# Masked cross-attention layer: two pairs of PSUM banks for scores instead of three, four ring banks instead of two, and scores later in TensorE's queue

## The chip, the cores and the metric

The kernel runs on one core of a Trainium2 chip as one program. The metric is the device time of one execution in microseconds (us); lower is better.

## What is computed

Four layers run one after the other over x of shape (4, 1024, 256), with a context of 77 keys. Layer 0 is causal attention and an MLP, layer 1 linear attention with a window, layer 2 the masked cross-attention, layer 3 a cross-attention with 16 heads of 64. The change touches layer 2 only:

```python
q = (queries @ Wq.T + bq).reshape(B, Nq, h, d).transpose(0, 2, 1, 3)      # h = 16, d = 16
k = (keys @ Wk.T + bk).reshape(B, -1, h, d).transpose(0, 2, 1, 3)         # 77 keys
v = (values @ Wv.T + bv).reshape(B, -1, h, d).transpose(0, 2, 1, 3)
scores = jnp.einsum('bhqd,bhkd->bhqk', q, k) / jnp.sqrt(jnp.float32(d))
scores = scores * attention_weights
scores = jnp.where(attention_mask, -jnp.inf, scores)
p_attn = jax.nn.softmax(scores, axis=-1)
out = jnp.einsum('bhqk,bhkd->bhqd', p_attn, v)
out = out.transpose(0, 2, 1, 3).reshape(B, Nq, D)
out = out @ Wo.T + bo
x = queries + out                                                         # then a layer norm
```

## The kernel before

`masked_context` (from line 1651) computes layer 2. Its unit is a tile of 128 tokens; there are 8 in each of 4 batches. For a tile, all 16 heads times 77 keys lie side by side in one row of 1232 scores, worked in two halves m of 616. A half is a unit (b, i, m), numbered 0 to 63. The steps of a tile, each a token in the queue of its engine:

- `scores` (TensorE, line 1805): q times the block-diagonal keys `kbd`, into a pair of PSUM banks of 308 columns each. `scores_of` gives the pair, number modulo 3: banks 0 to 5.
- `take` (VectorE, line 1959): multiplies the half in place by the weights `fs`, loaded by DMA.
- `low` (TensorE, line 1816): adds the mask, made to bf16 by `lower` on ScalarE (line 1906), onto the same banks.
- `shift` (VectorE, lines 1968 and 1972): maximum of each head, then scores less maximum into `pr` in SBUF. After it the pair of banks is free.
- `exp` (ScalarE, line 1913).
- `turned`, three groups of transposes of `pr` (TensorE, line 1867; evacuated to `pT` by ScalarE, line 1939).
- `att` (TensorE, line 1877: 20 small matmuls of `pT` with the values `V`; VectorE, lines 2005 and 2008: reciprocal of the sums and product).
- `flat` (TensorE, line 1883; ScalarE, line 1945), `out` (TensorE, line 1889; VectorE adds it to x, line 2014), `stats` (VectorE, line 1978).

Once a batch come `V` (TensorE, line 1849), and for the batch after it the transposes of x, `turn` (line 1855), the projections `q` (line 1861), on GpSimd the bias and the block-diagonal `kbd` and `vbd` (lines 1786 and 1777), and for the batch before it the layer norm (lines 1558 to 1592, with its root on GpSimd). During the last batch 16 projections `next` (line 1837) for the following layer run as well.

The order of each engine's queue is fixed ahead of time: `masked_schedule` gives each token a time in units of half a tile, and each engine's list is sorted by it. A token waits only by semaphores, and every engine works its list strictly in order.

PSUM has eight banks. Six hold scores. All other TensorE results (`k`, `v`, `V`, `turn`, `q`, `turned`, `att`, `flat`, `out`, `next`) go in turn through the ring of banks 6 and 7; class `Banks` makes a token wait until the one that used its bank before, two tokens earlier, is emptied by VectorE or ScalarE. `scores` waits for the `shift` of the unit three back.

Of the kernel before, what the change touches and what calls it, by code (L numbers as in the profile page):

```python
# [278 lines left out]
def build(nc, a, out):  # L279
    with ExitStack() as whole:  # L280
# [25 lines left out]
        front_layers(nc, a, sem, start, x, ident, identb, (below, near), ctxT, banks, masked)  # L306
        clear(nc, list(sems.values())[before:])
        masked_context(nc, a, sem, masked, folded, x, ident, identb, ctxT, banks)
        folded_context(nc, a, sem, folded, masked, x, ident, ctxT, banks, out)
        clear(nc, early)  # L310
# [1181 lines left out]
def masked_schedule():  # L1492

    pe, dve, act, pool, sp = [], [], [], [], []

    def fill(time, token, engine, after=0.3):

        pe.append((time, token))
        {"v": dve, "s": act}[engine].append((time + after, token))

    for m in range(ND):
        fill(-9 + m / 10, ("k", m), "v")
        fill(-8.5 + m / 10, ("v", m), "v")
    for b in range(B):
        t0 = UNITS * b
        for m in range(ND):
            pool.append((t0 - 6.5 + m / 10 if b else -7 + m / 10, ("keys", b, m)))
            pool.append((t0 - 6 + m / 10 if b else -6 + m / 10, ("vals", b, m)))
        fill(t0 + 1.2, ("V", b), "v")
        early = t0 - 9 if b else -5  # L1510
        for half in range(2):
            for k in range(ND):
                fill(early + 2 * half + k / 2, ("turn", b, half, k), "vs"[k])
            for m in range(ND):
                fill(early + 2 * half + 1.3 + m / 2, ("q", b, half, m), "s")
            pool.append((early + 2 * half + 1.5, ("bias", b, half)))
        for i in range(NT):
            for m in range(2):
                n = t0 + 2 * i + m
                u = (b, i, m)  # L1520
                pe += [(n - 1.4, ("scores", *u)), (n + 0.3, ("low", *u))]
                dve += [(n, ("take", *u)), (n + 1.1, ("shift", *u))]
                act.append((n + 1.6, ("exp", *u)))
            at = t0 + 2 * i
            sp.append((at - 6, ("side", b, i)))
            act.append((at - 1.6, ("lower", b, i)))
            for j in range(3):
                fill(at + 3.3 + j / 5, ("turned", b, i, j), "s")
            fill(at + 4.55, ("att", b, i), "v", 0.5)
            fill(at + 5.6, ("flat", b, i), "s")  # L1530
            fill(at + 6.4, ("out", b, i), "v", 0.5)
            dve.append((at + 7.2, ("stats", b, i)))
        end = t0 + UNITS + 5.7
        if b + 1 < B:
            norm_tokens(b, end, 0.5, dve, act, pool)

    for n in range(2 * NPAIR):
        fill(57 + 0.8 * n, ("next", n), "s")
    return [[token for _, token in sorted(steps, key=lambda step: step[0])] for steps in (pe, dve, act, pool, sp)]


def norm_tokens(b, at, pace, dve, act, pool):

    dve.append((at, ("spread", b)))
    pool.append((at + 0.05, ("root", b)))
    for i in range(NT):
        dve += [(at + 1 + pace * i, ("norm", b, i)), (at + 1.6 + pace * i, ("close", b, i))]
        act.append((at + 2.2 + pace * i, ("square", b, i)))
    dve.append((at + 3 + pace * NT, ("mean", b)))
    pool.append((at + 3.05 + pace * NT, ("mean_root", b)))  # L1550
# [100 lines left out]
def masked_context(nc, a, sem, t, folded, x, ident, identb, ctxT, banks):  # L1651

    nbuf = NBUF
    RING = (6, 7)
    wq, wk, wv, wo, bq, bk_, bv, bo, gamma, beta = (t[n] for n in ("wq", "wk", "wv", "wo", "bq", "bk", "bv", "bo",
                                                                   "gamma", "beta"))
    xT, qT, kv, kbd, vbd, heads, pick, ones, V = (t[n] for n in ("xT", "qT", "kv", "kbd", "vbd", "heads", "pick", "ones",
# [1 line left out]
    fs, mk, low, pr, pT, att, attT, top, inv = (t[n] for n in ("fs", "mk", "low", "pr", "pT", "att", "attT", "top",  # L1659
                                                               "inv"))  # L1660
# [5 lines left out]
             "mean", "mean_root", "newton", "chain")  # L1666
    side = [sem(f"side{n}") for n in range(nbuf)]
    pe_order, dve_order, act_order, pool_order, sp_order = masked_schedule()
    in_ring = lambda t: t[0] in ("k", "v", "V", "turn", "q", "turned", "att", "flat", "out", "next")
    of = lambda order, *kinds: [t for t in order if t[0] in kinds]  # L1670
    ring = Banks(banks, RING, [t for t in pe_order if in_ring(t)], sem("ring_ready"),
                 (Tally(sem("emptied_v"), [t for t in dve_order if in_ring(t)]),
                  Tally(sem("emptied_s"), [t for t in act_order if in_ring(t)])))
    scored, lowed = Tally(sem("scored"), of(pe_order, "scores")), Tally(sem("lowed"), of(pe_order, "low"))
    taken, shifted = Tally(sem("taken"), of(dve_order, "take")), Tally(sem("shifted"), of(dve_order, "shift"))
# [3 lines left out]
    number = {u: n for n, u in enumerate((b, i, m) for b in range(B) for i in range(NT) for m in range(2))}  # L1679
    unit = list(number)  # L1680
# [2 lines left out]

    def scores_of(u):

        r = 2 * (number[u] % 3)
        return banks[:, r:r + 2, 0:UW // 2]

    def by_head(ap):
# [5 lines left out]
    with nc.Block() as block:  # L1695
        @block.sync
        def _(sp):
            for _, b, i in sp_order:
                n = tile_of(b, i)
                if n < nbuf:  # L1700
                    continue
                if n == NT:
                    folded_loads(sp, a, sem, folded)
                sp.wait_ge(*taken.after(("take", *tiles[n - nbuf], 1)))
                sp.wait_ge(*lowered.after(("lower", *tiles[n - nbuf])))
                side_inputs(sp, a, sem, t, b, i)
            sp.wait_ge(loaded, 16 * nload)
            for done in side:
                sp.wait_ge(done, 32 * B * NT // nbuf)
# [80 lines left out]
        def _(pe):  # L1790
            for token in pe_order:
                what, *args = token
                if what == "scores":
                    b, i, m = args
                    n = number[b, i, m]
                    if n >= 3:
                        pe.wait_ge(*shifted.after(("shift", *unit[n - 3])))
                    if i % 4 == 0:
                        pe.wait_ge(*ring.emptied(("q", b, i // 4, m)))
                    if i == 0:  # L1800
                        pe.wait_ge(*keys_ready.after(("keys", b, m)))
                    for j in range(2):

                        rows = slice(P // 2 * j, P // 2 * (j + 1))
                        ins = pe.matmul(scores_of((b, i, m))[:, j], qT[rows, b % 2, m, i * P:(i + 1) * P],
                                        kbd[rows, b % 2, m, j * UW // 2:(j + 1) * UW // 2], start=True, stop=True,
                                        skip_group_check=True)
                    ins.then_inc(sem("scored"), 1)
                    continue
                if what == "low":  # L1810
                    b, i, m = args
                    pe.wait_ge(*taken.after(("take", b, i, m)))
                    pe.wait_ge(*lowered.after(("lower", b, i)))
                    for j in range(2):
                        c0 = m * UW + j * UW // 2
                        ins = pe.matmul(scores_of((b, i, m))[:, j], identb[:],
                                        low[:, tile_of(b, i) % 3, c0:c0 + UW // 2], start=False, stop=True,
                                        skip_group_check=True)
                    ins.then_inc(sem("lowed"), 1)
                    continue  # L1820
# [10 lines left out]
                elif what == "next":  # L1831
                    n, = args
# [116 lines left out]
        def _(dve):  # L1949
            chain = Chain(dve, sem("chain"))  # L1950
            for token in dve_order:
                what, b, *args = token
                if what == "take":
                    i, m = args
                    n = tile_of(b, i)
                    dve.wait_ge(*scored.after(("scores", b, i, m)))
                    dve.wait_ge(side[n % nbuf], 32 * (n // nbuf + 1))
                    two = scores_of((b, i, m))
                    dve.tensor_tensor(two, two, half_of(fs[:, n % nbuf, :], m).rearrange("p (a c) -> p a c", a=2),
                                      ALU.mult).then_inc(sem("taken"), 1)  # L1960
                    continue
# [450 lines left out]
```

## Time and profile before

| | |
|---|---|
| median of 3 runs | 2225.31 us (2221.91 to 2230.49) |
| profiled execution, its own time | 2232.05 us |
| its span, first to last instruction | 2230.3 us |
| mean granted TensorE clock | 0.971 |
| busy share of TensorE, VectorE, ScalarE, GpSimd | 90%, 62%, 51%, 34% |
| masked layer within the span | about 1557 to 1877 us |

Times in the rows are us from the start of the span. PE is TensorE's matmuls, PEld its weight loads, DVE is VectorE, ACT ScalarE, POOL GpSimd. PEclk is the granted clock as a share of 2.4 GHz. A row with xN stands for N instructions in a run; its second number is the time from the start of the first to the end of the last.

### The profile page before, as it was taken

How to read it: one execution, taken by the hardware profiler on the slowest of the kernel's cores; microseconds unless marked ns; L12 is line 12 of the kernel's file. 1: busy time of each engine (PE TensorE's matmuls, PEld its weight loads, DVE VectorE, ACT ScalarE, POOL GpSimd, SP SyncE). 2: the span in 40 equal slices, each digit the busy share in tenths (PEclk: the TensorE clock that was granted, in tenths of full speed). 3: DMA queues.
4: the chain of work that ended last, by engine and by line, in shares of the span. 5: the costliest groups of instructions: out<-in, count | busy, mean ns of one | idle time of the engine just before them, and what ended most of it. 6: DMA issues, size and time to landing. Idle time of an engine off the chain costs nothing. (4 is left out here: it accounts for less than half of the span.)

```text
span 2230.3 us, 38605 instructions
## 1 busy us (share of the span) xinstructions
PE 2013.3 (90%) x14610; PEld 1309.0 (59%) x14610; DVE 1386.9 (62%) x3054; ACT 1137.6 (51%) x1750; POOL 769.4 (34%) x1012
## 2 busy tenths in 40 slices
PE   4999999999998879998999899998989998999989
PEld 2333433343342258876566575765666667888989
DVE  4876776685767655645545554451677884866655
ACT  2265565555545666651645545363445553555444
POOL 3023124113212353311624526253111201756656
PEclk8799999999998999998999999999999999999999
DMA  6705403510730000018460716320422210000000
GB/s 146 140 7 113 60 1 68 89 23 36 113 76 1 1 15 1 1 55 122 92 108 21 143 17 131 66 66 1 162 86 86 85 58 1 11 10 13 16 13 20
DMA packets 77774, 126.68 MB, mean 57 GB/s; under 512 B 16650, under 2 KB 34826, under 8 KB 77582
## 3 DMA queue, kind: packets, MB, share of 16 engines
q1 hardware_dynamic: 74966, 122.63, 26.0%
q8 instruction: 118, 1.93, 0.4%
q10 hardware_dynamic: 2624, 1.58, 0.2%
q14 instruction: 66, 0.54, 0.1%
HBM read 93.59 MB, written 30.32 MB: 56 GB/s over the span
## 5 line engine op out<-in xcount | busy, mean ns | idle before, releaser
L1099 DVE TENSOR_REDUCE nmx_causal<-banks 128x1 f32<-128x333 f32 (+4 forms) x896 | 435.6, 538 | 174.1 <-PE banks L830 172.3
L988 ACT ACTIVATE probs_causal<-banks 128x1024 f32<-128x1024 f32 (+5 forms) x384 | 330.8, 899 | 258.3 <-PE banks L855 254.4
L830 PE MATMUL banks<-ks_causal,qs_causal 96*128 96x333 bf16 (+4 forms) x896 | 271.7, 339 | 13.8 <-DVE nmx_causal L1099 7.6
L753 POOL TENSOR_SCALAR_AFFINE_SELECT probs_window<-probs_window 128x512 f32<-128x512 f32 (+1 forms) x272 | 162.0, 602 | 258.0 <-ACT probs_window L988 247.0
L753 POOL TENSOR_SCALAR_AFFINE_SELECT probs_causal<-probs_causal 128x512 f32<-128x512 f32 (+2 forms) x160 | 92.4, 578 | 455.7 <-ACT probs_causal L988 455.4
L855 PE MATMUL banks<-qs_causal,ks_causal 97*128 97x512 bf16 (+5 forms) x896 | 209.6, 329 | 19.8 <-ACT probs_causal L988 16.0
L1099 DVE TENSOR_REDUCE nmx_window<-banks 128x2 f32<-128x384 f32 (+2 forms) x320 | 143.0, 460 | 104.5 <-PE banks L830 100.8
L879 PE MATMUL banks<-probs_causal,v_causal 128*17 128x512 f32 (+5 forms) x1792 | 185.8, 488 | 0.0
L988 ACT ACTIVATE probs_window<-banks 128x768 f32<-128x768 f32 (+2 forms) x128 | 99.7, 785 | 102.6 <-PE banks L855 102.1
L828 PEld LDWEIGHTS banks<-below,identb 128*128 128x128 bf16 x512 | 49.4, 98 | 173.5 <-DVE nmx_causal L1099 125.2
L830 PEld LDWEIGHTS banks<-ks_causal,qs_causal 96*128 96x128 bf16 x896 | 86.5, 99 | 103.5 <-DVE nmx_causal L1099 60.9
L828 PE MATMUL banks<-below,identb 128*128 128x128 bf16 x512 | 116.6, 231 | 31.8 <-DMA ks_causal<-zk 14.7
L2234 POOL TENSOR_TENSOR pT_folded<-full_folded,pT_folded 128x512 fp32r<-128x512 f32 (+1 forms) x96 | 107.0, 1135 | 89.2 <-ACT pT_folded L2338 88.9
L855 PEld LDWEIGHTS banks<-qs_causal,ks_causal 97*128 97x128 bf16 (+1 forms) x896 | 75.3, 101 | 92.8 <-ACT probs_causal L988 44.5
L2273 PE MATMUL banks<-vw_folded,pT_folded 128*128 128x256 f32 x960 | 125.8, 284 | 0.0
L346 PE MATMUL banks<-fold_folded,xT_folded 128*128 128x308 f32 x768 | 120.6, 306 | 4.0 <-DVE pr_folded L2359 3.9
L828 PE MATMUL banks<-near,identb 128*128 128x192 bf16 (+1 forms) x512 | 112.9, 251 | 11.1 <-DMA ks_window<-zk 6.2
L879 PE MATMUL banks<-probs_window,v_window 128*17 128x192 f32 (+3 forms) x1664 | 105.6, 333 | 17.7 <-ACT oT_window L999 14.0
L2273 PEld LDWEIGHTS banks<-vw_folded,pT_folded 128*128 128x128 f32 x960 | 115.6, 189 | 0.0
L346 PEld LDWEIGHTS banks<-fold_folded,xT_folded 128*128 128x128 f32 x768 | 110.3, 188 | 5.1 <-DVE pr_folded L2359 4.9
L830 PE MATMUL banks<-ks_window,qs_window 96*128 96x192 bf16 (+1 forms) x512 | 112.2, 249 | 0.0
L855 PE MATMUL banks<-qs_window,ks_window 97*128 97x192 bf16 (+2 forms) x832 | 101.7, 249 | 4.1 <-DMA qs_window<-nmT_window 4.1
(261 smaller groups left out, 4099.9 us busy)
## 6 DMA issues: line engine op xcount, KB each, us to landing
fs_masked<-in_fside SPq DMA_DIRECT2D x32, 616.0 KB, 3.7
ks_causal<-zk SPq DMA_DIRECT2D x96, 137.6 KB
ks_window<-zk SPq DMA_DIRECT2D x96, 137.6 KB
qs_causal<-zq SPq DMA_DIRECT2D x96, 128.0 KB
qs_window<-zq SPq DMA_DIRECT2D x96, 128.0 KB
zk<-parts_causal SPq DMA_DIRECT2D x24, 275.2 KB, 2.9
zk<-parts_window SPq DMA_DIRECT2D x24, 275.2 KB, 2.4
zq<-parts_causal SPq DMA_DIRECT2D x24, 256.0 KB, 6.9
```

What stands on the lines that cost most here:

```text
L346: ins = pe.matmul(out, left, right, start=n == 0, stop=n == len(terms) - 1)
L753: pool.affine_select(out=v, in_=v, compare_op=ALU.is_ge, fill=0.0, base=const, pattern=[[0, QH], [by_c, wd]], channel_multiplier=by_p).the ...
L828: pe.matmul(bk[:, to:to + mn], identb[:], mask[:, m0:m0 + mn], start=True, stop=False, skip_group_check=True)
L830: ins = pe.matmul(bk[:, c:c + m], qs[q][0:KR, h, t * P:(t + 1) * P], ks[q][0:KR, h, key:key + m], start=cover is None, stop=True, skip_gro ...
L855: ins = pe.matmul(banks[0:nk, at + side, o:o + n], ks[q][0:kr, 2 * pair + side, key:key + nk], qs[q][0:kr, 2 * pair + side, q0:q0 + n], st ...
L879: ins = pe.matmul(banks[32 * h:32 * h + DH + 1, OUT, query:query + n], v1[0:rows, blk, QH * q + h, :], probs[0:rows, at % 3, h // 2, h % 2 ...
L988: ins = act.activation(dst, src, ACT.Exp, scale=DH ** -0.5)
L1099: dve.tensor_reduce(dst, src, AX.X, ALU.max, negate=True).then_inc(emptied_v, 1)
L2234: pool.tensor_tensor(dst[:, 1], full[full_of(token)][:, 0:wd], dst[:, 0].bitcast(F32), ALU.subtract).then_inc(sem("lows"), 1)
L2273: ins = pe.matmul(out_of(b, i), pT[:, term[0], n % 2, c, :], vw[:, term[1], c, :], start=c == 0 and term == PARTS[0], stop=c == NPC - 1 an ...
```

## The change

Unit n of the scores uses pair n modulo 2, banks 0 to 3, and waits for the shift of unit n-2. The ring has banks 4 to 7. In `masked_schedule` the time of `scores` goes from n - 1.4 to n - 0.5, which moves it later in TensorE's queue only; no other queue changes.

```diff
@@ masked_schedule
-                pe += [(n - 1.4, ("scores", *u)), (n + 0.3, ("low", *u))]
+                pe += [(n - 0.5, ("scores", *u)), (n + 0.3, ("low", *u))]
@@ masked_context
-    RING = (6, 7)
+    RING = (4, 5, 6, 7)
@@ scores_of
-        r = 2 * (number[u] % 3)
+        r = 2 * (number[u] % 2)
@@ TensorE's block
-                    if n >= 3:
-                        pe.wait_ge(*shifted.after(("shift", *unit[n - 3])))
+                    if n >= 2:
+                        pe.wait_ge(*shifted.after(("shift", *unit[n - 2])))
```

## Rows read from the trace of the kernel before

**Rows 1.** Busy time by stretches: four batches, tail; then single periods. Columns in the first line.

```profile
core 0: us, PE busy (x) PEld busy (x) DVE busy (x) ACT busy (x) POOL busy (x), PEclk, DMA share, GB/s
1557.30:1626.83 69.53, 63.09 (x363) 43.04 (x363) 41.65 (x66) 33.54 (x53) 14.51 (x9) 0.93 0.43 141
1626.83:1706.81 79.98, 72.31 (x440) 52.44 (x439) 61.38 (x111) 40.10 (x78) 14.96 (x30) 0.94 0.24 79
1706.81:1781.54 74.73, 69.09 (x440) 50.15 (x439) 59.85 (x111) 40.36 (x78) 15.00 (x30) 0.98 0.26 86
1781.54:1842.49 60.95, 56.55 (x380) 42.94 (x379) 49.02 (x99) 34.14 (x70) 4.82 (x24) 1.00 0.20 66
1842.49:1877.00 34.51, 31.49 (x181) 23.72 (x180) 13.62 (x27) 13.58 (x30) 1.32 (x1) 1.00 0.00 0
...
1616.77:1626.83 10.06, 8.48 (x49) 6.62 (x49) 5.87 (x10) 4.18 (x7) 0.00 (x0) 0.83 0.31 85
...
1646.21:1653.51 7.30, 6.87 (x50) 5.33 (x49) 5.87 (x10) 4.18 (x7) 0.00 (x0) 1.00 0.35 110
...
1738.68:1752.57 13.89, 11.60 (x61) 7.50 (x60) 13.20 (x21) 6.76 (x15) 7.83 (x5) 0.88 0.18 57
```

**Rows 2.** Who waited for whom in the masked layer: total us, times, longest.

```profile
DVE inv_masked L2005 <- PE banks L1877: 31.3, 27, 2.4
```

**Rows 3.** Time line of TensorE's matmuls in one plain period: start, us, instruction.

```profile
1646.21 0.79 PE L1805 MATMUL banks<-kbd_masked,qT_masked 64*128 64x308 f32 x4
1646.93 0.66 PE L1867 MATMUL banks<-ident,pr_masked 128*128 128x128 f32 x4
1647.42 0.43 PE L1816 MATMUL banks<-low_masked,identb 128*128 128x308 bf16 x2
1647.68 0.60 PE L1867 MATMUL banks<-ident,pr_masked 128*128 128x128 f32 x4
1648.27 0.44 PE L1883 MATMUL banks<-ident,att_masked 128*128 128x128 f32 x2
1648.64 0.79 PE L1805 MATMUL banks<-kbd_masked,qT_masked 64*128 64x308 f32 x4
1649.86 0.44 PE L1867 MATMUL banks<-ident,pr_masked 128*128 128x128 f32 x2 [0.43 <-ACT pT_masked L1939]
1650.14 0.43 PE L1816 MATMUL banks<-low_masked,identb 128*128 128x308 bf16 x2
1650.40 1.02 PE L1889 MATMUL banks<-wo_masked,attT_masked 128*128 128x256 f32 x4
1651.26 2.32 PE L1877 MATMUL banks<-V_masked,pT_masked 128*128 128x51 f32 x20
1653.51 0.79 PE L1805 MATMUL banks<-kbd_masked,qT_masked 64*128 64x308 f32 x4
```

**Rows 4.** Time line of VectorE in the same plain period.

```profile
1646.31 0.26 DVE L2005 RECIPROCAL inv_masked<-banks 128x16 f32<-128x16 f32 x1 [1.01 <-PE banks L1877]
...
1646.95 0.79 DVE L1968 TENSOR_REDUCE top_masked<-banks 128x8 f32<-128x616 f32 x1
1647.77 0.80 DVE L1972 TENSOR_TENSOR pr_masked<-banks,top_masked 128x616 f32<-128x616 f32 x1
...
1648.82 0.79 DVE L1959 TENSOR_TENSOR banks<-banks,fs_masked 128x616 f32<-128x616 f32 x1
1649.52 0.79 DVE L1968 TENSOR_REDUCE top_masked<-banks 128x8 f32<-128x616 f32 x1
```

**Rows 5.** Time line: `q`, a flat and a third transpose group of 10.06, V, a bank wait.

```profile
1602.44 1.88 PE L1861 MATMUL banks<-xT_masked,wq_masked 128*128 128x512 f32 x4
...
1620.43 0.44 PE L1883 MATMUL banks<-ident,att_masked 128*128 128x128 f32 x2 [1.58 <-ACT pT_masked L1939]
...
1621.52 0.54 PE L1867 MATMUL banks<-ident,pr_masked 128*128 128x128 f32 x2
...
1637.60 2.66 PE L1849 MATMUL banks<-pick_masked,vbd_masked 128*128 128x51 f32 x22
...
1743.01 0.66 PE L1867 MATMUL banks<-ident,pr_masked 128*128 128x128 f32 x4 [1.94 <-DVE xT_masked L2000]
```

## Prediction

> **What bounds the kernel now.** I read the page first (TensorE is busy for 90% of the span), then the busy time by stretches, cut at the first scores matmul of each batch and of single tiles [rows 1]. The masked layer runs from 1557 to 1877 us, and only there does the change act. Its unit is a tile of 128 tokens, and I call the time from one tile's first scores matmul to the next one's a period. A period with no extra work takes 7.30 us, with TensorE busy for 6.87 of it and the clock at 1.00. Periods that also carry transposes and projections of the next batch take 12 to 14 us.
>
> The time lines of a plain period say what sets those 7.30 us. On TensorE [rows 3] read the starts: scores of half 0 at 1646.21, of half 1 at 1648.64, the third transpose group at 1649.86 behind 0.43 us of waiting for ScalarE, then low, out, the attention product `att` at 1651.26, and the next tile at 1653.51. On VectorE [rows 4] read what it waits for: its reciprocal, the first instruction of `att`, stands still 1.01 us for the end of TensorE's `att`, and behind it in the queue stands the shift of half 0. Over the layer VectorE waits 31.3 us in 27 places like this one [rows 2]. So a ring of dependences sets the period: scores half 1, third transposes, low, out, `att` on TensorE (1648.64 to 1651.26 + 2.32 = 1653.58), `att` on VectorE (0.64, from 1646.31 to 1646.95), the shift of half 0 (1.62, from 1646.95 to 1647.77 + 0.80), and 0.07 us later the next tile's scores half 1, which waited for that shift, as it is three units back. 4.94 + 0.04 + 0.64 + 1.62 + 0.07 = 7.31, the period. TensorE's ring of two banks adds to it only through the 0.43 us.
>
> **The change part by part.** No instruction is added or removed. Three things change: (a) scores wait for the shift two units back instead of three; (b) `scores` stands 0.9 units later in TensorE's queue; (c) turns, projections and outputs have four banks. The orders of VectorE, ScalarE, GpSimd and SyncE stay as they are, so nothing moves past another step there, DMA triggers included.
>
> Sorted by the new times TensorE's queue for a plain tile i is: scores(i,0), flat(i-3), turned(i-2,2), low(i,0), out(i-3), scores(i,1), att(i-2), turned(i-1,0), low(i,1), turned(i-1,1), and again. VectorE's is: take(i,0), shift(i-1,1), out(i-3), take(i,1), att(i-2), shift(i,0), stats(i-3). I lay one on the other with durations and start-to-start steps of [rows 3, 4], from 0 at scores(i,0):
> - Scores end at 0.79. Take runs from 0.83 to 1.63 (0.04 to be released, as between `att` and the reciprocal). TensorE is through flat (0.37) and turned (0.28) by 1.4 and waits at low until 1.68. This wait is new: low used to stand far behind its scores.
> - shift(i-1,1) follows take 0.70 later, 1.53 to 3.16. scores(i,1) must wait for it: it starts at 3.22, though TensorE had finished out's issue at 2.80. This wait is new too.
> - `att` starts 0.72 later at 3.94 and ends at 6.26. VectorE's `att` runs from 6.30, the shift of (i,0) from 6.94 to 8.56, and the next tile's scores, which now wait for this very shift, start at 8.62. TensorE has had nothing to do since 7.4 (3.94 + `att` 2.25 + transposes 0.49 + low 0.26 + transposes 0.49 = 7.43).
>
> So the plain period becomes 8.6 us instead of 7.30: the loop now holds both scores and a take in series with `att`. What (c) removes, the 0.43 us and the shorter waits at flat, is no longer on that loop and gives nothing there. It does give something elsewhere. From tile 4 of batch 0 to tile 0 of batch 1 exp precedes the first evacuation in ScalarE's queue; in tile 7 flat waits 1.58 us for it [rows 5] and the period is 10.06 [rows 1]; with four banks flat doesn't wait, and these also fall to 8.6. In the tiles with turns a transpose group waits 1.94 us for VectorE's copy of `xT` [rows 5]; that goes too.
>
> Now by periods, in each batch numbered 0 to 7.
> - Period 1 carries V: 22 matmuls, 2.66 us [rows 5]. In the new queue they stand behind `att`, where 1.2 us are free, so 8.6 + 2.5 - 1.2 = 9.9.
> - Period 3 carries the statistics of the batch before (batches 1 to 3): aggregates before take and a norm that waits for GpSimd's root before take(3,1); `att` starts some 0.6 later: 9.2. In batch 0 it stays near 8.7.
> - Period 4: two transpose groups and two projections q of 1.88 us each [rows 5], and 1.8 each start to start. For batches 1 and 2, five short VectorE steps stand before take, so low is at 3.4, q and out end their issue at 6.3, scores and `att` at 9.25, q, turn, transposes and low at 12.65: TensorE's queue sets it. Batch 0, without norms: 11.5.
> - Period 5: the same count with one transpose group fewer and take 0.8 us late: 11.4; batch 0: 10.7.
> - Periods 0, 2, 6, 7: 8.6 each, as the last q now lies in period 5.
> - Periods 4 to 6 of batch 3, with eight of the `next` projections in their slack: 9.8, 10.8, 8.95.
> - The ramp, periods 0 to 2 of batch 0: with two pairs, take, shift and scores alternate with nothing between; the same laying out brings tile 3 at 22.4 us after 1557.3 where it was at 17.7.
>
> Batch 0: 22.4 + 8.7 + 11.5 + 10.7 + 8.6 + 8.6 = 70.5, before 69.53, +1.0. Batches 1 and 2: 8.6 + 9.9 + 8.6 + 9.2 + 12.65 + 11.4 + 8.6 + 8.6 = 77.6. To this comes the slowing of norm steps while GpSimd works: in [rows 1] period 4 has 21 VectorE instructions in 13.20 us where a plain one has 10 in 5.87. Most of that lies under TensorE's 12.65; I put 1 us, from 0 to 4. 78.6 is -1.4 against 79.98 and +3.9 against 74.73. Batch 3 up to its last tile: 8.6 + 9.9 + 8.6 + 9.2 + 9.8 + 10.8 + 8.95 = 65.9, +4.9 against 60.95. The tail is TensorE at 31.49 of 34.51 us; it begins with 2.3 us of its work done and loses some 0.5 of bank waits: -2.8. The head (first projections) may give 0.5. Sum: 1.0 - 1.4 + 3.9 + 4.9 - 2.8 - 0.5 = **+5 us** at full clock.
>
> **The clock.** The row of the 10.06 us period shows a granted clock of 0.83, that is some of it at 1.2 GHz instead of 2.4, with TensorE busy for 8.48 us, 84%, and one gap of 1.58 us; the plain ones, with gaps of 0.43, stay at 1.00. From the third transposes to the next tile it took 5.31 us there (1621.52 to 1626.83, [rows 1, 5]) and 3.65 in the plain one (1649.86 to 1653.51): 1.66 us lost. The new plain period would have 6.9 busy in 8.6, 80%, with gaps of 1.2, 0.3 and 0.4 close together, all in front of what lies on the loop. Some 16 periods are of this kind. Bounds: none falls, 0; all do, 27 us. I take a third of them, 9 us, as the gaps are shorter than 1.58 but come in a cluster. The Trainium skill ("TensorE: Matmul & The Clock Gate", section "A second HAM failure mode: psum-queue depth-cycling") tells of a kernel whose small idles between groups of matmuls made the clock swing between its two levels; by it the upper bound, +32 in all, would be the case. The 10.06 us period agrees, the plain one of before doesn't.
>
> **The sum.** +5 + 9 = +14 us. Against the profiled execution's own 2232.05 (span 2230.3 and 1.75 around it) that is 2246. The median of the runs shown is 6.7 lower, 2225.31, and I move by the same: **2240**.
>
> **The rivals.**
> - *The loop at full clock* (+5 and up to 10 less if the mixed periods lose more than I gave them): 2220 to 2233. For it: the plain periods keep 1.00 now. Decides if no plain period shows a lower clock.
> - *The clock falls in every plain period*: +32, 2257, to 2270 if it falls twice. For it: the 84% row; against: the gaps here are each shorter.
> - *The ring was what cost, and the change wins*: if VectorE's `att` and shift ran far enough ahead of the scores' waits, only the waits for banks would count. They go: some 0.8 us of TensorE waiting in each of 16 plain periods and 10 us in the mixed ones: -23, 2202. It decides from the point where shift(i,0) ends before TensorE is through turned(i-1,1), 7.4 us in my laying out; it ends at 8.56, so 1.2 us speak against it. The Trainium skill ("Perfetto Trace Analysis", section "Matmuls") asks that independent matmul groups rotate through banks so that evacuation overlaps the next group; by that alone this would be the outcome. The 0.43 and 1.58 us waits agree that the ring waits; the 1.01 us of VectorE's waiting for `att` says that the scores' banks are needed more.
> - *The change does less than it says*: none here, as the waits are written by hand; both orders are fixed.
>
> **How the numbers follow.** Forecast (2233 to 2250) 0.52; loop at full clock 0.22; clock everywhere 0.18; ring wins 0.08. A measurement of this kernel can tell about 0.5%, 11 us, from no change: 2214.2 to 2236.4. Slower: 0.44 of the forecast case and all of the clock case, 0.62. Faster: most of the last case, 0.07. Same: the rest, 0.31. The range for 8 in 10 leaves out the ring case and the top of the clock case: 2219 to 2264.
>
> **What would show it.** Right: plain periods of 8.6 us; scores waiting for `pr_masked` of VectorE before both halves, over 1 us for half 0; low waiting for take; VectorE's wait before the reciprocal grown from 1.0 to about 1.4; the waits of transposes for ScalarE gone; tile 7 of batch 0 shorter than 10.06; granted clock below 1.00 in some plain periods. Wrong: plain periods at or under 7.3, which would mean that the shift isn't behind `att`; or mixed periods well under 11 us, which would mean that I counted TensorE's queue there too long.

## The result

| | before | after |
|---|---|---|
| median | 2224.31 us (2221.91 to 2230.49, 4 runs) | 2258.27 us (2246.47 to 2264.82, 4 runs) |
| profiled execution, its own time | 2232.05 us | 2264.82 us |
| its span | 2230.3 us | 2263.0 us |
| mean granted clock | 0.971 | 0.963 |
| first projection of the masked layer to first matmul of the folded layer | 1543.0 to 1875.7, 332.7 us | 1552.5 to 1909.9, 357.4 us |

The changed kernel is slower: 2258.27 / 2224.31, a ratio of 1.0134 with a 95% interval of 1.0107 to 1.0161, +34 us (forecast 2240, range 2219 to 2264). The spans differ by 32.7 us, in three pieces: +9.5 us before the masked layer, +24.7 us in it, -1.5 us behind it. The first and the last lie in code that the change doesn't touch. Over the twelve profiles of this study, of kernels that are all alike ahead of this layer, it starts between 1541.2 and 1557.2 us, so one pair of executions can differ there by 16 us. The profiles therefore say +24.7 us, and what the medians say beyond it (34) is put to no part of the change. Part of that excess lies in the runs of before: the second set of runs of the changed kernel, told below, has 17 runs of before beside it with a median of 2232.23 us, and there the difference is 26 us. From here on I read the masked layer alone.

Busy time by stretches of the kernel after, cut as in [rows 1]: four batches and the tail, then the ramp (tiles 0 to 2 of batch 0), a plain period, the period with V in batches 1 and 3, period 4 of batch 1 and period 4 of batch 3.

```profile
core 0: us, PE busy (x) PEld busy (x) DVE busy (x) ACT busy (x) POOL busy (x), PEclk, DMA share, GB/s
1567.52:1640.62 73.10, 63.87 (x369) 43.99 (x369) 44.70 (x71) 32.31 (x53) 13.73 (x8) 0.91 0.42 144
1640.62:1725.63 85.01, 71.81 (x438) 51.35 (x438) 61.25 (x112) 40.74 (x80) 14.56 (x30) 0.94 0.23 75
1725.63:1810.70 85.07, 71.63 (x439) 51.23 (x439) 61.17 (x112) 40.48 (x79) 14.94 (x30) 0.94 0.23 75
1810.70:1881.67 70.97, 63.09 (x382) 47.22 (x383) 49.82 (x100) 35.22 (x72) 4.80 (x24) 0.90 0.14 45
1881.67:1911.00 29.33, 27.43 (x166) 21.96 (x166) 11.57 (x23) 12.13 (x27) 1.12 (x1) 1.00 0.00 1
...
1567.52:1591.61 24.09, 19.28 (x98) 13.19 (x97) 13.71 (x19) 8.99 (x13) 4.32 (x2) 0.75 0.29 99
1631.90:1640.62 8.72, 7.17 (x48) 5.12 (x49) 6.06 (x11) 3.96 (x8) 0.00 (x0) 1.00 0.27 91
1640.62:1652.87 12.25, 11.88 (x70) 9.59 (x70) 7.03 (x12) 5.14 (x9) 0.00 (x0) 0.80 0.22 66
1810.70:1820.62 9.92, 9.37 (x70) 7.60 (x70) 6.84 (x12) 4.26 (x8) 0.00 (x0) 1.00 0.25 80
1680.08:1696.97 16.89, 12.71 (x65) 8.09 (x65) 14.72 (x22) 7.62 (x19) 7.41 (x5) 0.90 0.19 64
1847.57:1862.69 15.12, 13.87 (x52) 10.11 (x52) 10.88 (x23) 7.00 (x17) 0.00 (x0) 0.56 0.03 10
```

Batches 0 to 3 take 73.10, 85.01, 85.07 and 70.97 us, where they took 69.53, 79.98, 74.73 and 60.95 [rows 1]. The plain period is 8.72 us instead of 7.30, with the clock at 1.00. The last line of the first group reaches a microsecond into the folded layer: the tail itself went from 33.2 to 28.2 us.

Who waited for whom after, from 1557 to 1900 us (total us, times, longest), against [rows 2]:

```profile
DVE inv_masked L2005 <- PE banks L1877: 48.9, 31, 3.6
DVE banks L1959 <- PE banks L1805: 42.0, 51, 4.9
PE banks L1805 <- DVE pr_masked L1972: 23.0, 33, 1.2
PE banks L1816 <- DVE banks L1959: 19.1, 23, 4.3
```

VectorE's waiting for `att` rose from 31.3 to 48.9 us (50.6 if the last 10 us of the layer are counted in). TensorE's scores wait for the shift (23.0 us) and its low waits for take (19.1 us): in each pair of lines the two engines wait for each other in turn. VectorE's wait for scores stood at 5.6 us in 2 places before.

The time line of the plain period shows the loop, TensorE and VectorE together (start, us, instruction, and in brackets the wait ahead of it). It is tile 7 of batch 0, from its scores of half 0 to those of the next tile:

```profile
1631.90 0.79 PE L1805 MATMUL banks<-kbd_masked,qT_masked 64*128 64x308 f32 x4 [1.18 <-DVE pr_masked L1972]
1632.74 0.81 DVE L1959 TENSOR_TENSOR banks<-banks,fs_masked 128x616 f32<-128x616 f32 x1 [0.56 <-PE banks L1805]
1633.61 0.44 PE L1816 MATMUL banks<-low_masked,identb 128*128 128x308 bf16 x2 [0.33 <-DVE banks L1959]
1634.28 0.80 DVE L1972 TENSOR_TENSOR pr_masked<-banks,top_masked 128x616 f32<-128x616 f32 x1
1635.13 0.79 PE L1805 MATMUL banks<-kbd_masked,qT_masked 64*128 64x308 f32 x4
1635.85 2.42 PE L1877 MATMUL banks<-V_masked,pT_masked 128*128 128x51 f32 x20
1638.31 0.26 DVE L2005 RECIPROCAL inv_masked<-banks 128x16 f32<-128x16 f32 x1 [1.53 <-PE banks L1877]
1639.77 0.80 DVE L1972 TENSOR_TENSOR pr_masked<-banks,top_masked 128x616 f32<-128x616 f32 x1
1640.62 0.79 PE L1805 MATMUL banks<-kbd_masked,qT_masked 64*128 64x308 f32 x4 [1.18 <-DVE pr_masked L1972]
```

Scores of half 0, take, the shift behind it and scores of half 1 take 3.23 us, start to start. Then scores of half 1 let `att` go on TensorE, that lets the reciprocal go (after 1.53 us of waiting; 1.01 in [rows 4]), behind it in VectorE's queue stands the shift, and that lets the next tile's scores go at 1640.62, after 1.18 us in which TensorE did nothing: 5.49 us. 3.23 and 5.49 are the 8.72. The wait of half 1 for the shift is short: the row of its matmuls shows no idle time ahead, and that of its weight load shows 0.44 us behind VectorE.

### The profile page after: what moved, and what is told of

Its sections match the earlier page's. It is cut to its first block and busy times, and to the rows that moved or that the text cites. A ratio compares the mean times of both kernels' runs of the same rounds, so it can differ in the third digit from the quotient of the medians.

```text
span 2263.0 us, 38605 instructions
## 1 busy us (share of the span) xinstructions
PE 2025.5 (90%) x14610; PEld 1313.4 (58%) x14610; DVE 1389.8 (61%) x3054; ACT 1138.1 (50%) x1750; POOL 768.4 (34%) x1012
## 5 line engine op out<-in xcount | busy, mean ns | idle before, releaser
L828 PE MATMUL banks<-near,identb 128*128 128x192 bf16 (+1 forms) x512 | 113.1, 251 | 11.4 <-DMA ks_window<-zk 6.6
```

The costliest lines, as they stand in the source:

```text
L828: pe.matmul(bk[:, to:to + mn], identb[:], mask[:, m0:m0 + mn], start=True, stop=False, skip_group_check=True)
```

## The experiments

Each comparison is with runs of the kernel before on the same chip. "Layer" is the stretch of the masked layer as in the table above: 332.7 us before, 357.4 after.

**The kernel after once more**, to see how far the layer repeats on another chip.

> The changed kernel itself, unaltered, beside the others of this call. In the profiled executions the two layers ahead of the masked one, which the change doesn't touch, took 9.5 us longer in the changed kernel. If that is how executions differ, the start of the masked layer lies anywhere from 1541 to 1557 us and the layer itself again at 357 us, within 4; if it came with the change, the start is again near 1552. Period 4 of batches 1 and 2 near 17 us, those of batch 3 near 10 or 15 by the clock.

Measured: 2258.52 us, ratio 1.011 (1.0065 to 1.0155); layer 360.9 us, from 1546.2 us on. So the late start of 1552.5 us didn't come with the change. The layer of one kernel varies by 3.5 us between two executions, and differences of that size between layers below decide nothing. Here they come with the granted clock: period 3 of batches 2 and 3 took 10.39 and 10.79 us at 0.84, where the first execution had 9.16 and 9.51 at 1.00, and period 4 of batch 2 took 18.47 at 0.82 instead of 17.23 at 0.90.

**The ring back at two banks, the rest of the change kept.**

```diff
-    RING = (4, 5, 6, 7)
+    RING = (6, 7)
```

> The changed kernel with the ring of two banks of before; two pairs for scores and the late scores stay, banks 4 and 5 lie idle. Theory of the loop (scores, take, shift, scores of the other half, att on TensorE, att on VectorE, shift): no wait for a ring bank lies on the loop, so plain periods stay at 8.7 us and the masked layer within 5 us of the changed kernel, longer only where a turn or a projection waits for its bank. Rival, that the four banks carry a gain which hides a larger loss: plain periods 9.2 us or more and the total over 10 us longer than the changed kernel.

Measured: 2264.33 us, ratio 1.0122 (1.0076 to 1.0169); layer 363.3 us; plain periods 8.72 us as with four banks. So with two pairs the ring is on no loop of the plain period, and four banks bring the layer from 363.3 to 357.4 or 360.9 us, some 2 to 6 us. Against the first of these, batch 0 gives 5.1 us (78.23 to 73.10), the tail 3.0 and the head 1.0. Batches 1 and 2 give nothing (85.00 and 84.25 us with the ring of two, 85.01 and 85.07 with four): what period 3 gains there, 11.46 to 9.16 us in batch 1, period 4 loses again, 14.33 to 16.89. Batch 3 loses 2.3 us, as its period 4 has a granted clock of 0.56 with four banks and 0.84 with two. The rival in which the ring wins falls. By the Trainium skill ("Perfetto Trace Analysis", section "Matmuls"), whose advice is to rotate independent groups of matmuls through banks, a gain was due here. The trace agrees in the head, in batch 0, in period 3 and in the tail; the plain period doesn't move by 0.01 us.

**The order alone: the kernel before with scores later in TensorE's queue.** Three pairs and two ring banks stay.

```diff
-                pe += [(n - 1.4, ("scores", *u)), (n + 0.3, ("low", *u))]
+                pe += [(n - 0.5, ("scores", *u)), (n + 0.3, ("low", *u))]
```

> The kernel of before with scores at n - 0.5 in TensorE's queue; three pairs and the ring of two stay. Theory of the loop: scores no longer wait for a shift, but take and low now lie between scores and att: att on VectorE 0.64, shift 1.55 to the next start, stats 0.33, take 0.85, low 0.28, out 0.86, scores 0.72, att on TensorE 2.36, together 7.6 us a plain period, 0.3 above before, so about 5 us on the total, 2230. Of the 1.4 us that a plain period gained, 1.1 would then come from the second pair's wait. Rival, that the late place of scores is the cause: 8.7 us and most of the 34 us.

Measured: 2254.72 us, ratio 1.0102 (1.0072 to 1.0132); layer 346.7 us, +14.0. Two plain periods of it (7.47 and 8.22 us) by stretches, and behind them lines of the second one's time line:

```profile
1639.15:1646.62 7.47, 7.07 (x49) 5.07 (x48) 4.77 (x8) 3.89 (x7) 0.00 (x0) 1.00 0.25 73
1646.62:1654.84 8.22, 7.12 (x50) 5.10 (x49) 5.96 (x11) 4.18 (x7) 0.00 (x0) 1.00 0.31 112
```

```profile
1648.81 0.44 PE L1867 MATMUL banks<-ident,pr_masked 128*128 128x128 f32 x2 [1.03 <-ACT pT_masked L1939]
...
1650.30 0.79 PE L1805 MATMUL banks<-kbd_masked,qT_masked 64*128 64x308 f32 x4
1651.02 2.42 PE L1877 MATMUL banks<-V_masked,pT_masked 128*128 128x51 f32 x20
...
1653.48 0.26 DVE L2005 RECIPROCAL inv_masked<-banks 128x16 f32<-128x16 f32 x1 [1.53 <-PE banks L1877]
```

The order costs more than I expected of it. `att` now stands behind the scores of half 1 on TensorE, so VectorE waits 1.53 us for it even where the scores wait for nothing. The ring of two banks adds 1.03 us ahead of the third transposes. So of the +24.7 us in the layer, 14.0 are there with the order alone. The second pair's wait accounts for the rest: from this kernel to the one with two pairs and two ring banks the layer goes from 346.7 to 363.3, +16.6, and the two more ring banks return 2 to 6 of them. The split is rough. The layer of 346.7 us is that of this kernel's fastest execution, and by the medians, all taken on the same chip, the order costs 23.0 us and the second pair's wait 9.6 (2231.74, 2254.72 and 2264.33 us). Both readings give each of the two a share; neither settles which is the larger.

**Two pairs with the scores left early.** The other parts of the change are kept.

```diff
-                pe += [(n - 0.5, ("scores", *u)), (n + 0.3, ("low", *u))]
+                pe += [(n - 1.4, ("scores", *u)), (n + 0.3, ("low", *u))]
```

> The changed kernel with scores at n - 1.4 as before; two pairs and the ring of four stay. Theory of the loop: scores of half 1 wait for the shift of the other half at 3.2 us, and third transposes, low, out and att now stand behind that wait: att ends at 7.7, att on VectorE and the shift at 10.0, so plain periods of 10.0 us and a total some 20 us above the changed kernel, about 2280. The theory that the late place of scores costs time says the opposite: below the changed kernel.

Measured: 2363.42 us, ratio 1.0549 (1.0499 to 1.0599); layer 459.9 us. A plain period by stretches, and from the time line the scores of another tile:

```profile
1810.24:1821.71 11.47, 8.21 (x48) 6.27 (x48) 6.07 (x11) 4.09 (x7) 0.00 (x0) 0.80 0.22 69
```

```profile
1725.51 1.40 PE L1805 MATMUL banks<-kbd_masked,qT_masked 64*128 64x308 f32 x4 [2.35 <-DVE pr_masked L1972]
```

The direction is as expected, the size isn't: 2280 was expected. With two pairs the later place in the queue is needed: scores placed early hold up everything behind them for 2.35 us. On top of that the clock is at 0.80, and the same four scores matmuls take 1.40 us instead of 0.79.

**VectorE's `att` behind the shift**, in the kernel after. If the shift is late only because it queues behind `att`, one changed number should take `att` off the loop. The last argument of `fill` is how much later than TensorE's part VectorE's stands; at 0.5 `att` of tile i comes just ahead of the shift of (i+2,0), at 0.6 just behind it.

```diff
-            fill(at + 4.55, ("att", b, i), "v", 0.5)
+            fill(at + 4.55, ("att", b, i), "v", 0.6)
```

> The changed kernel with one step moved in VectorE's queue: att stands behind the shift of half 0 instead of ahead of it. Theory of the loop: the shift no longer waits for TensorE's att, TensorE's own queue sets the period (shift of the other half 3.16, scores 3.22, att 3.94, transposes, low and transposes to 7.45): plain periods 7.45 us instead of 8.72, some 16 to 18 of them, the total 20 us below the changed kernel, about 2237. Rival, that TensorE's bank waits or its clock set the period: no change.

Measured: 2232.62 us, ratio 0.9988 (0.9958 to 1.0017); layer 325.7 us. Stretches of a plain period and of period 4 of batch 1, then the wait line, to be held against the one of after:

```profile
1643.93:1651.40 7.47, 6.91 (x50) 5.14 (x49) 5.96 (x10) 4.18 (x9) 0.00 (x0) 1.00 0.34 118
1659.45:1677.32 17.87, 13.68 (x65) 8.54 (x64) 15.86 (x26) 7.61 (x20) 7.41 (x5) 0.81 0.22 76
```

```profile
DVE inv_masked L2005 <- PE banks L1877: 5.5, 3, 2.1
```

The plain period falls from 8.72 to 7.47 us (expected 7.45), the wait for `att` from 48.9 to 5.5 us, and the layer by 31.7 us. This shows the loop as told: `att` was in it through its place in VectorE's queue. Period 4 stays long (17.87 us), so it has another cause.

**The same number in the kernel before.**

```diff
-            fill(at + 4.55, ("att", b, i), "v", 0.5)
+            fill(at + 4.55, ("att", b, i), "v", 0.6)
```

> The kernel of before with one step moved in VectorE's queue: att behind the shift of half 0. Theory of the loop: the plain period of 7.30 us was set by TensorE's att, VectorE's att, the shift and the next scores; with the shift free of att, TensorE's own steps of 6.5 us are left and some bank waits: 6.7 us a plain period, and the 10 us periods at the end of batch 0 fall below 8. The masked layer 10 to 15 us below before's 332.7. Rival, that the ring of two banks or VectorE's sum of work (5.9 us a tile) bound the tile in any case: plain periods stay at 7.3 and the total stays.

Measured: 2214.04 us, ratio 0.9918 (0.9886 to 0.9949); layer 312.6 us. It is faster than both kernels. The plain period as time line:

```profile
1637.77 0.80 DVE L1972 TENSOR_TENSOR pr_masked<-banks,top_masked 128x616 f32<-128x616 f32 x1
1637.94 0.79 PE L1805 MATMUL banks<-kbd_masked,qT_masked 64*128 64x308 f32 x4
1638.48 0.25 DVE L2005 RECIPROCAL inv_masked<-banks 128x16 f32<-128x16 f32 x1
...
1640.01 0.44 PE L1883 MATMUL banks<-ident,att_masked 128*128 128x128 f32 x2
1640.38 0.79 PE L1805 MATMUL banks<-kbd_masked,qT_masked 64*128 64x308 f32 x4
1641.10 0.44 PE L1867 MATMUL banks<-ident,pr_masked 128*128 128x128 f32 x2
...
1644.74 0.53 PE L1805 MATMUL banks<-kbd_masked,qT_masked 64*128 64x308 f32 x2
```

The reciprocal follows the shift and waits for nothing. The period is 6.80 us, and its busy time on TensorE is 6.80 too: the loop is gone and TensorE's own work is the bound.

Beside [rows 3] these lines also say where the 0.50 us had been. TensorE's steps follow each other at the same distances in both kernels, within 0.01 us, but for one: the third transposes start 0.72 us behind scores of half 1 here (1640.38 to 1641.10), and 1.22 us behind them in [rows 3] (1648.64 to 1649.86). Scores of half 1 start 0.37 us after flat in both (1640.01 and 1648.27), although here the shift had ended long before, at 1638.57. So in the kernel before, the shift didn't hold these scores up by anything that the rows show. What came late was a ring bank. Two lines of ScalarE in the kernel before, `exp` and an evacuation of transposes:

```profile
1648.61 0.72 ACT L1913 ACTIVATE pr_masked<-pr_masked 128x616 f32<-128x616 f32 x1 [0.39 <-DVE pr_masked L1972]
1649.23 0.58 ACT L1939 ACTIVATE pT_masked<-banks 128x512 f32<-128x512 f32 x1
```

`exp` waits for the late shift. Behind it in ScalarE's queue stands the evacuation of the second transposes, which ends at 1649.81, and the third transposes, two tokens later in the ring of two and so in the same bank, start at 1649.86. From the third transposes over TensorE's `att`, VectorE's `att`, the shift, `exp` and this evacuation back to the third transposes are 3.72 + 0.04 + 0.64 + 1.62 + 0.04 + 0.62 + 0.58 + 0.05 = 7.31 us, the period. So the loop of the kernel before closes through ScalarE's queue and a ring bank, and not through a pair of the scores. This is read from the rows; no run isolates it, since the edit of `att` takes both paths apart.

The wait of flat behind exp is gone as well: tile 7 of batch 0, 10.06 us in [rows 1], now takes 6.80.

**Period 4 of batches 1 and 2.** It takes 16.89 and 17.23 us, forecast 12.65 and 1 for GpSimd. The time line of batch 1 in the kernel after:

```profile
1680.08 0.79 PE L1805 MATMUL banks<-kbd_masked,qT_masked 64*128 64x308 f32 x4 [0.74 <-DVE pr_masked L1972]
1681.53 2.35 POOL L1786 TENSOR_TENSOR x_tokens<-x_tokens,bo_masked 128x1024 f32<-128x1024 f32 x1 [5.86 <-PE banks L1855]
1681.65 2.51 DVE L1565 SCALAR_TENSOR_TENSOR x_tokens<-x_tokens,mv_masked,gamma_masked 128x256 f32<-128x256 f32 x1
1683.84 2.75 POOL L1777 TENSOR_TENSOR kbd_masked<-kv_masked,heads_masked 128x616 f32<-128x616 f32 x2
1684.08 1.43 DVE L1569 SCALAR_TENSOR_TENSOR x_tokens<-x_tokens,sd_masked,beta_masked 128x256 f32<-128x256 f32 x1
1685.44 0.79 DVE L1959 TENSOR_TENSOR banks<-banks,fs_masked 128x616 f32<-128x616 f32 x1
1686.29 0.69 PE L1816 MATMUL banks<-low_masked,identb 128*128 128x308 bf16 x2 [3.84 <-DVE banks L1959]
```

GpSimd's bias starts 1.45 us after the tile's scores, as soon as the second transposes of x are through. Two norm steps of VectorE, which stand ahead of take, run beside it and beside the block-diagonal keys behind it, and take 2.51 and 1.43 us instead of 0.48; take is late, and TensorE's low waits 3.84 us for it, with the whole queue behind. Before, in batch 2, the bias started 5.51 us after the scores of 1738.68 [rows 1]:

```profile
1744.19 2.36 POOL L1786 TENSOR_TENSOR x_tokens<-x_tokens,bo_masked 128x1024 f32<-128x1024 f32 x1 [6.27 <-PE banks L1855]
```

The ring of two had held the transposes up: in the kernel with two pairs and two ring banks period 4 takes 14.33 and 14.73 us, less than with four, though the period ahead of it takes 11.46 and 11.52 instead of 9.16. To test the cause, the bias waits. First for take of (4,0), then for the take behind the norms, (5,1):

```diff
+                    if b and half == 0:
+                        pool.wait_ge(*taken.after(("take", b - 1, 4, 0)))
```

> The changed kernel with one wait more on GpSimd: the bias of the next batch's first half waits for take of tile 4, so that it and the block-diagonal keys and values no longer run beside the norm steps that stand ahead of that take. Theory: period 4 of batches 1 and 2 was 17 us instead of 13 since the freed ring lets GpSimd start 4 us earlier, where its work slows VectorE's norm steps to 1.4 to 2.5 us while low waits for take. Expected: period 4 at 13 to 14.5, the others as before, the total 5 to 8 us below the changed kernel. Rival, that the slow norm steps are only moved behind take and cost the same there: no change.

Measured: 2254.41 us, ratio 1.0096 (1.0058 to 1.0134); layer 354.4 us. Period 4 fell to 13.28 and 13.31 us, but period 5 rose from 11.23 to 15.91 and 15.85: the bias met the next norm steps. The sum of both periods, 29.2, isn't below the 28.1 of after; the saving I expected missed. The layer is 3.0 us shorter all the same, through the periods with V: they took 9.93, 9.93 and 9.92 us, each at a granted clock of 1.00. The place was wrong, not yet the cause, so the wait was moved:

```diff
+                    if b:
+                        pool.wait_ge(*taken.after(("take", b - 1, 5, 1)))
```

> The changed kernel with both biases on GpSimd waiting for take of tile 5, half 1, which stands behind all norm steps: nothing of GpSimd's large steps then runs beside them. Theory: the contention costs periods 4 and 5 of batches 1 and 2 together 28.1 us instead of the 24 (12.7 and 11.3) of TensorE's queue; delaying the bias only to take of tile 4 moved it on to period 5 (13.3 and 15.9). Expected: norm steps at 0.48 us throughout, periods 4 and 5 together 24 to 25, the masked layer 6 to 9 us below the changed kernel. Rival, that these periods are long because of TensorE's slower clock behind low's wait for take: 28, as before.

Measured: 2246.15 us, ratio 1.0062 (1.0038 to 1.0086); layer 346.2 us, 11.2 below after. The instructions of the layer norm's line 1565 (ns least/median/most), first in the kernel after:

```profile
L1565 DVE SCALAR_TENSOR_TENSOR x_tokens<-x_tokens,mv_masked,gamma_masked x24: 473/477/2574, 1675.7 to 1865.9; 128x256 f32<-128x256 f32 x24
```

Then in this one, and its period 4 of batch 1 by stretches:

```profile
L1565 DVE SCALAR_TENSOR_TENSOR x_tokens<-x_tokens,mv_masked,gamma_masked x24: 473/475/486, 1666.1 to 1845.4; 128x256 f32<-128x256 f32 x24
```

```profile
1670.44:1683.06 12.62, 11.43 (x65) 7.53 (x65) 10.68 (x22) 7.48 (x19) 0.00 (x0) 1.00 0.25 85
```

No norm step is slowed any more, and periods 4 and 5 take 12.62 and 11.22 us, the 12.65 and 11.4 of the forecast without contention. VectorE is busy for 10.68 us in place of 14.72 and GpSimd has nothing in that stretch. This settles the cause of the long period 4. In batches 1 and 2 it is 8.9 us shorter, most of the 11.2; the rest lies where the two executions differ in clock, in period 4 of batch 3 above all (10.73 us at 0.84 instead of 15.12 at 0.56). Part of the saving in period 4 of batches 1 and 2 comes with the clock too, 0.90 before the wait and 1.00 with it. On the slowed steps the Trainium skill ("SBUF — State Buffer", section "Who interferes with whom") says that a VectorE instruction with two inputs in SBUF contends with a GpSimd instruction that reads SBUF, for a port pair that the two engines share and that is locked exclusively. The trace agrees: the norm step that started 0.12 us after the bias ends at 1684.16, only 0.28 us after the bias did (1683.88).

**Both edits together**, first on the kernel after (`att` at 0.6, bias behind take of (4,0)):

```diff
-            fill(at + 4.55, ("att", b, i), "v", 0.5)
+            fill(at + 4.55, ("att", b, i), "v", 0.6)
...
+                    if b and half == 0:
+                        pool.wait_ge(*taken.after(("take", b - 1, 4, 0)))
```

> The changed kernel with both edits: att behind the shift of half 0 on VectorE, and the bias on GpSimd behind take of tile 4. If the two causes are separate, the gains add: plain periods 7.47, period 4 of batches 1 and 2 from 17.5 to about 13, the masked layer 317 us against 325.7 with the first edit alone and 332.7 before, so a total about 0.5% below before. If not, it equals the first edit alone.

Measured: 2225.64 us, ratio 0.998 (0.9957 to 1.0002); layer 325.2 us, where `att` alone had 325.7: no further gain, a miss. Periods 4 and 5 fell to 14.09 and 11.58 us (from 17.87 and 10.91), but the periods with V took 11.76, 9.93 and 11.14 us, where `att` alone had 9.93, 9.93 and 9.92. The granted clock goes with them: 0.84, 1.00 and 0.88, where `att` alone had 1.00 three times. Why it fell isn't settled.

Then on the kernel before (`att` at 0.6, bias behind take of (5,1)):

```diff
-            fill(at + 4.55, ("att", b, i), "v", 0.5)
+            fill(at + 4.55, ("att", b, i), "v", 0.6)
...
+                    if b:
+                        pool.wait_ge(*taken.after(("take", b - 1, 5, 1)))
```

> The kernel of before with both edits: att behind the shift of half 0 on VectorE, both biases on GpSimd behind take of tile 5. If the contention with GpSimd costs something in the kernel of before too, periods 4 and 5 of batches 1 and 2, 26.9 and 25.0 us with the first edit alone, fall to 24 or less, where the bank waits for VectorE's copies allow it, and the masked layer from 312.6 to about 307. If its cover there was complete, nothing changes.

Measured: 2213.59 us, ratio 0.9932 (0.9906 to 0.9958); layer 315.9 us against 312.6 without the wait: no gain, another miss. Periods 4 and 5 take 26.2 us in batch 1 and 26.1 in batch 2, where `att` alone had 26.9 and 25.0. With two ring banks TensorE waits in period 4 for banks anyway. Here is the stretch, and from its time line one group of transposes:

```profile
1721.27:1734.82 13.55, 11.51 (x62) 7.43 (x61) 11.38 (x23) 6.77 (x15) 0.00 (x0) 0.87 0.19 61
```

```profile
1724.28 0.66 PE L1869 MATMUL banks<-ident,pr_masked 128*128 128x128 f32 x4 [1.64 <-DVE att_masked L2010]
```

GpSimd is idle there, and the transposes still wait 1.64 us, now for VectorE's `att` to empty a bank. The best kernel of the study remains the one before with `att` at 0.6; the wait on top of it changes the median by less than 1 us.

## Why the prediction was right in direction and low in size

- **Plain period** (forecast 8.6): 8.72, with the waits where they were put: scores for the shift (1.18 us ahead of half 0), low for take (0.33), the reciprocal 1.53 (forecast some 1.4). The edit of `att` on VectorE shows the loop.
- **The loop of the kernel before** was told with a wrong last link. I closed it with the scores of half 1, which "waited for that shift", and said that the ring adds to it only through the 0.43 us. But the 4.94 us in that sum contain the 0.43; without it the sum is 6.88, no longer than the 6.87 us for which TensorE is busy anyway. The experiment on the kernel before shows these scores at the same place with the shift long done, and the rows close the loop through `exp`, an evacuation and a ring bank. So the 1.01 us of VectorE's waiting didn't say that the scores' banks were needed more. The forecast for the plain period didn't rest on this link: with two pairs the wait for a pair is written into the kernel, and it came (1.18 us).
- **The 10.06 us periods of batch 0** (8.6): 8.71 and 8.72. Right.
- **V** (9.9): 9.92 at full clock, in batch 3. I called it period 1; it lies in period 0. In batches 1 and 2 it took 12.25 and 11.96, at clocks of 0.80 and 0.82, and the period behind it 9.33 instead of 8.6, at 0.90 and 0.86: 3.1 and 2.8 us more than the two were given. It is the clock that makes the difference and not the queue: with the bias behind take of tile 4 the same period, behind the same waits of 1.18 and 0.33 us, keeps 1.00 and takes 9.93, 9.93 and 9.92 us.
- **Period 3** (9.2): 9.16 twice, 9.51 in batch 3; in batch 0 9.32 (8.7), at a clock of 0.91. **Period 5** (11.4): 11.23. Right.
- **Period 4 of batches 1 and 2** (12.65, plus 1 for GpSimd): 16.89 and 17.23. The queue of TensorE was laid out rightly (12.62 with the contention gone); the term for the norm steps was mis-sized. I took most of it as hidden under TensorE's work and put 1 us, and missed that the four ring banks, which free the transposes, bring the bias forward from 5.5 to 1.45 us after the scores, onto norm steps that stand ahead of take. It was 4.2 and 4.6 us over the 12.65, above the upper bound of 4 that I gave, and 6.8 us more than the forecast in both batches together.
- **The clock** (+9, put in 16 plain periods): in the wrong place. Ten plain periods are at 1.00 and take 8.72 us, so the rival in which it falls in every one is refuted; only the two behind a period with V are lower, 1.2 us in both. It fell in the ramp (0.75), in two of the periods with V and behind them, and in period 4 of batch 3 (0.56; 15.12 us for the 9.8 forecast, and the same again in the second execution). Over my values these make 1.7 + 0.6 (tile 3 of batch 0, 9.32) + 5.9 + 5.3 = 13.5 us. What the Trainium skill tells of another kernel, and the prediction weighed ("TensorE: Matmul & The Clock Gate", section "A second HAM failure mode: psum-queue depth-cycling"), isn't seen in these ten plain periods, which idle for 18% of their time in several small gaps.
- **Tail** (-2.8): -5.0. Better than forecast. **Head** (-0.5): +0.7.

The sum against the forecast at full clock (+5): batch 0 +2.6, batches 1 and 2 +6.4 and +6.5, batch 3 +5.1, tail -2.2, head +1.2, in all +19.6, which makes the +24.7 of the layer. 9 of the 19.6 stood in the forecast as the clock's. The other 10.6, the 9.5 us ahead of the layer and the -1.5 behind it, which belong to no part of the change, are what the profiled execution (2264.82) is above its forecast of 2246.

That the median of 2258.27 us lies inside the range is in part luck. The loop of the plain period was worked out and came as forecast. But the 9 us of the clock were put where hardly any were lost, and stand in the sum for losses in other periods; GpSimd's contention cost more than the bounds given for it; and a tail 2.2 us better than forecast hid some of it.

The row at a lower clock, period 4 of batch 3, with what the same matmuls cost there:

```profile
1852.53 1.40 PE L1805 MATMUL banks<-kbd_masked,qT_masked 64*128 64x308 f32 x4
1853.86 4.48 PE L1877 MATMUL banks<-V_masked,pT_masked 128*128 128x51 f32 x20
```

0.79 became 1.40 and 2.42 became 4.48 us. The price of the lower clock here is in the longer matmuls of the loop, not in the length of any wait. What pulls it down in this period and not in the plain ones stays open: no run isolated it. In the kernel after with `att` at 0.6 the same period keeps 1.00 and takes 9.76 us, near the 9.8 of the forecast.

## What to carry to other kernels

Before giving banks to one use or another, write down the loop that sets the period, and see which buffer is a link of it, for the count that it would have: with two pairs the scores' pairs were a link and the ring wasn't (8.72 us with either ring), and with three pairs the rows show the ring of two as the link. Check each link of the loop by the row of the instruction that is said to wait; one that starts at its usual distance from the step before it was held up by nothing. Look first for instructions which are in that loop only through their place in an in-order queue; one such step, moved behind its neighbour, was worth 1.25 us a tile with two pairs and 0.50 with three, without a bank. And when a buffer is made larger, ask which engine may now start earlier, and whom it will meet there.

## What was not expected of the hardware

- A norm step of VectorE (128x256, two tensors from SBUF) takes 0.48 us alone, and 1.43 and 2.51 us beside GpSimd's instructions of 1.4 and 2.35 us. The slowing is in the row of the victim alone: the bias of 2.35 us is as long as where nothing runs beside it. Only 3 of the 96 biases in the twelve profiles take 2.58 to 2.62 us.
- The granted clock doesn't follow the busy share of a tile: 1.00 at 82% (7.17 of 8.72 us), 0.83 at 84% in the 10.06 us period [rows 1], 0.80 at 72% (8.21 of 11.47 us) in the kernel with early scores, where the busy time itself is stretched by the clock. The waits just ahead don't decide it either: the period with V of batch 1 has 0.80 in the kernel after and 1.00 in the one with the bias behind take of tile 4, behind the same waits.
- Layers that no edit touches differ by up to 16 us between the twelve profiled executions, as told under the result.
